# Second feed-forward product made transposed, its residual added by VectorE on the way out of PSUM

## The reference

```python
for l in range(3):
    scores = leaky_relu(si[:, :, None] + sj[:, None, :] + attn_b[l])   # si, sj: x times a vector
    attn = softmax(where(mask, scores, -inf))
    h  = layernorm(x + attn @ x, g1[l], beta1[l])
    ff = gelu(h @ W1[l] + b1[l]) @ W2[l] + b2[l]                       # 256 -> 1024 -> 256
    x  = layernorm(h + ff, g2[l], beta2[l])
```

## Time and profile before

| | us |
|---|---|
| median of 3 runs (lowest, highest) | 2346.72 (2340.11, 2352.82) |
| the profiled execution, own time | 2341.39 |
| its span, first to last instruction | 2339.6 |
| PE busy, share | 2266.7, 97% |
| PE weight loads (PEld) busy, share | 2100.0, 90% |
| DVE busy, share | 2081.9, 89% |
| ACT busy, share | 1678.3, 72% |
| POOL busy, share | 1101.6, 47% |
| granted TensorE clock, mean | 0.993 |

### The profile page before, as it was taken

How to read it: one execution, slowest core, us unless ns; L and a number is a source line. 1 busy time by engine, 2 the same in 40 slices (tenths; PEclk the granted TensorE clock), 3 DMA queues, 4 the chain that set the end, 5 groups by cost and what they waited for, 6 DMA issues and landing times.

```text
span 2339.6 us, 44738 instructions
## 1 busy us (share of the span) xinstructions
PE 2266.7 (97%) x15900; PEld 2100.0 (90%) x15900; DVE 2081.9 (89%) x4844; ACT 1678.3 (72%) x2682; POOL 1101.6 (47%) x1319
## 2 busy tenths in 40 slices
PE   8999999997899999999999999999999999999997
PEld 7988888896899999899999999999998999999996
DVE  5998999999798989989999999999898999999875
ACT  3444444334788888788888888988888878788784
POOL 3556666565253443443434345344344564653521
PEclk9999999999999999999999999999999999999998
DMA  5665555466979777787575665765666657566431
GB/s 164 183 197 168 154 158 169 134 185 204 235 204 233 213 208 195 216 221 207 172 248 158 186 205 172 205 184 171 183 194 217 176 159 216 163 190 179 122 106 46
DMA packets 282815, 427.00 MB, mean 183 GB/s; under 512 B 89376, under 2 KB 183264, under 8 KB 282592
## 3 DMA queue, kind: packets, MB, share of 16 engines
q1 hardware_dynamic: 254944, 323.47, 44.5%
q0 software_dynamic: 27648, 100.68, 18.7%
HBM read 226.65 MB, written 79.99 MB: 131 GB/s over the span
## 4 chain that ended last, share of the span: by engine, by line
PE 57%; DVE 17%; ACT 9%; POOL 6%; DMA 5%; issue 4%; SPq 1%; DVEq 0%; ACTq 0%; POOLq 0%
PE A L1928 6%; PE A L1929 5%; PE A L1930 5%; PE PT L1959 4%; PE PT L1955 4%; PE PT L1956 4%; DVE t L1600 4%; PE Y L1969 3%; PE Y L1970 3%; PE Y L1971 3%; DVE g_lo L1689 2%; PE A L45 2%; PE A L46 2%; PE A L47 2%; ACT t L1461 2%
## 5 line engine op out<-in xcount | busy, mean ns | idle before, releaser
L1928 PE MATMUL A<-x_hi,pT_hi 128*128 128x258 f32 x1536 | 439.8, 286 | 7.5 <-DVE u L1619 4.3
L1969 PE MATMUL Y<-w,g_hi 128*128 128x256 f32 x1536 | 438.0, 285 | 6.6 <-DVE g_lo L1689 5.5
L1929 PE MATMUL A<-x_hi,pT_lo 128*128 128x258 f32 x1536 | 434.1, 283 | 0.0
L1930 PE MATMUL A<-x_lo,pT_hi 128*128 128x256 f32 x1536 | 431.9, 281 | 0.0
L1970 PE MATMUL Y<-w,g_hi 128*128 128x256 f32 x1536 | 430.6, 280 | 0.0
L1971 PE MATMUL Y<-w,g_lo 128*128 128x256 f32 x1536 | 430.1, 280 | 0.0
L1507 ACT ACTIVATE g<-PT,b 128x512 f32<-128x512 f32 x384 | 263.8, 687 | 219.6 <-PE PT L1959 215.8
L1363 POOL DMA_DIRECT2D t<-maskT x192 | 173.4, 946 | 399.4 <-DVE t L1600 392.6
L1607 DVE TENSOR_TENSOR pT_lo<-t,pT_hi 128x512 fp32r<-128x512 f32 x384 | 256.8, 684 | 80.5 <-ACT t L1461 80.0
L1689 DVE TENSOR_TENSOR g_lo<-g,g_hi 128x512 fp32r<-128x512 f32 x384 | 262.9, 685 | 66.3 <-ACT g_hi L1510 66.1
L1969 PEld LDWEIGHTS Y<-w,g_hi 128*128 128x128 f32 x1536 | 289.3, 188 | 28.3 <-DVE g_lo L1689 11.9
(11 more groups left out here) (196 smaller groups left out, 5791.9 us busy)
## 6 DMA issues: line engine op xcount, KB each, us to landing
t<-maskT POOLq DMA_DIRECT2D x192, 512.0 KB, 4.6
mask<-mask SPq DMA_DIRECT2D x192, 256.0 KB, 4.4
a_adj_t<-in_adj SPq DMA_DIRECT2D x64, 512.0 KB, 4.4
maskT<-turned SPq DMA_DIRECT2D x64, 512.0 KB, 5.0
rrow<-rline SPq DMA_DIRECT2D x96, 256.0 KB, 4.9
x_rows<-rows SPq DMA_DIRECT2D x24, 1024.0 KB, 7.7
mask<-a_mask SPq DMA_DIRECT2D x64, 256.0 KB, 4.6
turned<-maskT SPq DMA_DIRECT2D x32, 512.0 KB, 6.9
```

What stands on the lines that cost most here:

```text
L1928: pe.matmul(L.A[:, t, 0:DE], hi, L.x_hi[par][:, j, :], start=(j == 0), stop=False)
L1929: pe.matmul(L.A[:, t, 0:DE], lo, L.x_hi[par][:, j, :], start=False, stop=False)
L1930: mm = pe.matmul(L.A[:, t, 0:D], hi, L.x_lo[par][:, j, :], start=False, stop=(j == NT - 1))
L1969: pe.matmul(L.Y[:, t, :], hi, w2_part(0, f), start=False, stop=False)
```

## The change

`down` is turned: W2's 128x128 pieces are the stationary operand and the gelu's output, 512 columns, is the moving one. Two banks of `Y`, now called `YT[0]` and `YT[1]`, hold the product transposed (features on partitions, 512 rows in the free dimension). `down` has 6 matmuls of 512 columns in place of 12 of 256, its first four wait for the gelu alone and its last two for `g_lo`. `residual` is gone. A new VectorE step `sum_z` reads both banks, adds `h` and writes `zT`, which lies in the buffer `xo` that `n2` fills later. A new PE step `transpose_z` turns `zT` back into rows in `Y` with 8 transposes, inside `aggregate` of the chunk two further on, before its step j = 2. `stats2`, and `end` for the last chunk, wait for these. Waits for the earlier store of `xo` move from `n2` to `sum_z`; `h` waits for `sum_z` of the chunk before.

```diff
@@ scalar
             if m >= 1:
                 act.wait_ge(L.s_ffn1, KF * m)
+                act.wait_ge(L.s_zT, KD * m)
...
             act.wait_ge(L.s_rs2, 4 * (m + 1))
-            if m >= 2:
-                act.wait_ge(L.s_xst, 16 * (m - 1))
@@ vector
+        def sum_z(m):
+            dve.wait_ge(L.s_ffn2, KF * (m + 1))
+            if m >= 2:
+                dve.wait_ge(L.s_xst, 16 * (m - 1))
+                if layer_of(m - 2) < LAYERS - 1:
+                    dve.wait_ge(L.s_uv, 2 * TC * (m - 1))
+            for i in range(KD):
+                dve.tensor_tensor(L.zT[m % 2][:, i, :], L.YT[i][:, :], L.h[:, i, :], ALU.add).then_inc(L.s_zT, 1)
+
         def stats2(m):
-                if t == 0:
-                    dve.wait_ge(L.s_ffn2, KF * (m + 1))
+                if t % 2 == 0:
+                    dve.wait_ge(L.s_zT_turned, 2 * m + t // 2 + 1)
...
+                if old:
+                    sum_z(k - 2)
                 if agg:
-                    for j in range(LEAD, LEAD + 2):
+                    for j in range(LEAD, LEAD + 3):
                         p_lo(k, j)
                 if old:
                     stats2(k - 2)
...
+            sum_z(K - 1)
             for pair in range(2):
                 end(pair)
@@ tensor, aggregate
             for j in range(NT):
+                if k >= 2 and j == 2:
+                    transpose_z(k - 2)
...
-        def residual(m):
...
+        def transpose_z(m):
+            pe.wait_ge(L.s_zT, KD * (m + 1))
             for t in range(TC):
                 for i in range(KD):
-                    pe.matmul(L.Y[:, t, i * P:(i + 1) * P], L.h[:, i, t * P:(t + 1) * P], L.ident[:, :],
-                              start=(t % 2 == 0 and i == 0), stop=False, is_transpose=True)
+                    mm = pe.transpose(L.Y[:, t, i * P:(i + 1) * P], L.zT[m % 2][:, i, t * P:(t + 1) * P], L.ident[:, :])
+                if t % 2 == 1:
+                    mm.then_inc(L.s_zT_turned, 1)
@@ tensor, down
+            pe.wait_ge(L.s_gelu, 2 * (n + 1))
+            for i in range(KD):
+                ds = slice(i * P, (i + 1) * P)
+                pe.matmul(L.YT[i][:, :], w2_part(0, f)[:, ds], hi, start=(f == 0), stop=False)
+                pe.matmul(L.YT[i][:, :], w2_part(1, f)[:, ds], hi, start=False, stop=False)
             pe.wait_ge(L.s_g_lo, n + 1)
-            for t in range(TC):
...
-                pe.matmul(L.Y[:, t, :], hi, w2_part(0, f), start=False, stop=False)
-                pe.matmul(L.Y[:, t, :], hi, w2_part(1, f), start=False, stop=False)
-                mm = pe.matmul(L.Y[:, t, :], lo, w2_part(0, f), start=False, stop=last and t % 2 == 1)
...
+            for i in range(KD):
+                ds = slice(i * P, (i + 1) * P)
+                mm = pe.matmul(L.YT[i][:, :], w2_part(0, f)[:, ds], lo, start=False, stop=(f == KF - 1))
+            mm.then_inc(L.s_ffn2, 1)
...
                 up(k - 1, 0)
                 up(k - 1, 1)
-                residual(k - 1)
...
+            transpose_z(K - 1)
```

More of the change, by code:

```diff
@@ L798, in layer_buffers @@
     L.A, L.G, L.Y, L.lines = mem.A, mem.G, mem.Y, mem.PT
+    L.YT = [mem.Y[:, 2 * i:2 * i + 2, :].rearrange("p a d -> p (a d)") for i in range(2)]
     L.half = sb("half", [P, TC])
@@ L859, in layer_buffers @@
     L.xo = [sb("xo0", [P, TC, D], F32, "probabilities"), sb("xo1", [P, TC, D], F32, "odd keys")]
+    L.zT = [xo[:, :, :].rearrange("p (i a) d -> p i (a d)", i=KD) for xo in L.xo]
     L.prod = sb("prod", [P, 2, D], F32, "probabilities")
@@ L918, in layer_buffers @@
     L.s_out = sem("out")
-    L.s_last_bank = sem("last_bank")
+    L.s_zT = sem("zT")
+    L.s_zT_turned = sem("zT_turned")
     L.s_end = sem("end_step")
@@ L1726, in end @@
             done = 1 + 12 * pair
-            dve.wait_ge(L.s_last_bank, pair + 1)
+            dve.wait_ge(L.s_zT_turned, 2 * K)
             for t in tiles:
@@ L1734, in end @@
             for t in tiles:
-                if t == 0:
-                    dve.wait_ge(L.s_xst, 16 * (K - 2))
                 dve.scalar_tensor_tensor(xo[:, t, :], L.Y[:, t, :], L.mv2[:, t, 0:1], L.g2[:, :], ALU.subtract,
@@ L1820, in rest @@
                 if agg:
-                    for j in range(LEAD + 2, NT - 1):
+                    for j in range(LEAD + 3, NT - 1):
                         p_lo(k, j)
@@ L1963, in down @@
             n = KF * m + f
-            pe.wait_ge(L.s_g_lo, n + 1)
-            last = f == KF - 1
-            for t in range(TC):
-                ts = slice(t * P, (t + 1) * P)
-                hi, lo = L.g_hi[:, n % G_RING, ts], L.g_lo[:, n % G_RING, ts]
-                pe.matmul(L.Y[:, t, :], hi, w2_part(0, f), start=False, stop=False)
-                pe.matmul(L.Y[:, t, :], hi, w2_part(1, f), start=False, stop=False)
-                mm = pe.matmul(L.Y[:, t, :], lo, w2_part(0, f), start=False, stop=last and t % 2 == 1)
[L1972 to L1975, removed]
+            if f == 0:
+                if m == 0:
+                    pe.wait_ge(stage.s_z, SLOTS)
+                else:
+                    pe.wait_ge(L.s_n2, TC * m)
+            hi, lo = L.g_hi[:, n % G_RING, :], L.g_lo[:, n % G_RING, :]
+            pe.wait_ge(L.s_gelu, 2 * (n + 1))
[3 more added lines that the diff above has]
+                pe.matmul(L.YT[i][:, :], w2_part(1, f)[:, ds], hi, start=False, stop=False)
+            pe.wait_ge(L.s_g_lo, n + 1)
+            for i in range(KD):
+                ds = slice(i * P, (i + 1) * P)
+                mm = pe.matmul(L.YT[i][:, :], w2_part(0, f)[:, ds], lo, start=False, stop=(f == KF - 1))
+            mm.then_inc(L.s_ffn2, 1)
         def beside(slot):
@@ L1992, in rest @@
                     aggregate(k)
+                if k == K:
+                    transpose_z(K - 2)
                 up(k - 1, 0)
                 up(k - 1, 1)
-                residual(k - 1)
                 for f in range(KF):
```

## The result

The changed kernel takes 2393.88 us (median of 4 runs, 2389.59 to 2402.25) against 2343.91 us of the kernel before (4 runs, 2340.11 to 2352.82): ratio 1.0217, 95% interval 1.0189 to 1.0245, so 2.2% slower. The forecast was 2407, the range 2374 to 2440. The profiled execution takes 2393.82 us, its span is 2392.0 against 2339.6.

The account below looks back on a forecast made before the run. The prediction took PE as the bound, with a chain through ACT and DVE within 0.2 us of its pace. Terms 29 + 23.5 + 4 + 9 = 65.5 us on 2341.4 gave 2407 us, range 2374 to 2440.

Parts of the forecast that it names:

- The chain of the first two layers: Low part, additions, transposes, then j = 2: +1.15 us in 29 of 33 iterations, 36.7 us against 35.57; sum +29.
- The four long ones: Four iterations of the first two layers, long because of transfers that the new wait partly hides: −1 us each.
- The additions: sum_z on DVE, two additions out of PSUM a chunk: 2 × 0.67 = 1.34 us, ends 1.2 and 1.5.
- `down` and the weight loads: down on PE: 1.38 us in both forms, half as many weight loads buy nothing; 0.1 us gained an iteration.
- The rival on weight loads: Weight loads set PE's pace, so sum_z hides: 2333 us, not slower; chance 0.11 with its weaker form.
- The last layer: 13 iterations, gelu held by POOL's late nmr: nine times 2.1 us and four times 1.15, +23.5.
- the two terms: Last layer where nmr is late: additions 1.34 us plus transposes 0.79 us, the whole 2.1 us stays.
- The clock: Last layer: PE's wait of about 2.7 us lowers the clock in half of 13 iterations, 1.5 us each, +9.
- the signs of being right: PE waits once an iteration before transpose_z, 1.3 to 1.5 us, last layer 2 to 3; iterations 36.7 and 38 us.
- The prediction's rival for the first two layers: Clock falls there too, half of 33 iterations losing 1.5 us: +25, so 2432 us; chance 0.21.
- a microsecond there is hidden: Delay of n2 behind stats2 costs nothing, as down(0) needs n2 only some 4 us after up(0) begins.
- The end: Last two chunks have no aggregate beside them; sum_z and transposes stand bare, 2.1 us twice: +4.

Follow-up runs that it names:

- Run 4: Kernel before plus the two additions (result unused) behind the third low part, PE waiting for them before j = 2; down and transposes as before; 2382.41 us.
- run 1: Changed kernel with the eight transposes of zT before step j = 3 of aggregate in place of j = 2; 2373.56 us.
- run 10: run 6 with row_top moved behind the last low part on DVE; 2355.0 us.
- run 9: Changed kernel with its two additions made twice; 2484.51 us.
- run 5: Changed kernel with its two additions made three times; 2599.76 us.
- run 2: Changed kernel with the additions in row_top's place on DVE and row_top behind the third low part; 2378.3 us.
- run 6: run 2 with the statistics of the second norm one low part earlier on DVE; 2367.48 us.

## Why the prediction was right, and where it failed

*The chain of the first two layers: right to 0.14 us at each point.* From the first of the three `down` (1220.72), with the forecast in brackets: low part ends at 7.82 (7.82), additions at 9.02 (9.16), j = 2 begins at 9.92 (9.95), `up(0)` at 18.54 (18.50), and the iteration is 1257.49 − 1220.72 = 36.77 (36.7). That the end fits better than the parts is luck: the additions came 0.14 early, and from their end to j = 2 it took 0.90 in place of 0.79. PE's wait itself was forecast too long: "about 1.4 us" is the whole of the additions, while the prediction's own points give 9.16 − 8.01 = 1.15, and 0.98 was measured. In 33 iterations +27.6 (29). The four long ones became 5.6 us shorter together (38.26, 39.48, 37.71 and 38.82 became 37.36, 37.74, 36.77 and 36.79; forecast 4): the new wait did hide part of the transfers. Runs 4 and 1 show the cause: the additions with PE's wait, without the rest of the change, make most of the loss, and moving only the place where PE waits takes 20 us back.

*The additions: 0.68 each, 1.28 for the pair* (forecast 1.34), since the second starts before the first has ended.

*`down` and the weight loads.* 1220.72 to 1222.10 is 1.38 us, as forecast. PEld fell from 33.42 us in an iteration to 31.13 in run 10, and the iteration stayed at 35.6, so the loads did not set the pace. The rival on weight loads is out. The Trainium skill ("Perfetto Trace Analysis", section "Identifying the Most-Contended Engine") takes the busy share of the weight loads, beside the share of peak arithmetic, as the measure of TensorE's headroom. From the kernel before to run 10 that share fell from 94% to 87% of the iteration and gave no time; the matmuls' own 1.38 us told it.

*The last layer: +21.4 against 23.5, by the mechanism named.* Timeline of POOL in one of its iterations; then of PE, from that iteration's `up(0)` on, with its first matmul after each wait (the last row opens the next iteration); then the window on the iteration, and ACT's wait for `nmr` in the whole layer:

```profile
1958.35 2.92 POOL L1330 TENSOR_TENSOR nmr<-nm,rstd 128x4 f32<-128x4 f32 x1
```

```profile
1945.08 0.40 PE L1966 MATMUL PT<-h_hi,w 128*128 128x512 f32 x1
...
1969.20 0.36 PE L1942 MATMUL A<-x_hi,pT_hi 128*128 128x258 f32 x1 [0.48 <-DVE pT_lo L1609]
...
1973.96 1.09 PE L1951 MATMUL Y<-ident,xo 128*128 128x128 f32 x8 [1.25 <-DVE xo L1642]
...
1986.76 0.50 PE L1966 MATMUL PT<-h_hi,w 128*128 128x512 f32 x1 [0.42 <-ACT g_hi L1512]
```

```profile
1945.08:1983.42 38.34, 36.45 (x212) 31.08 (x210) 34.69 (x74) 29.02 (x47) 21.00 (x19) 1.00 0.59 177
```

```profile
ACT u L1484 <- POOL nmr L1330: 18.3, 9, 2.0
```

`nmr` took 2.92 us in nine iterations, as before, and ended 16.2 us after `up(0)` (1945.08 to 1961.27), as before: POOL's chain did not come forward. ACT waited 18.3 us for it in the layer, 12.5 before. Eight of the nine came to 38.3 to 38.8 us, 2.0 to 2.5 over 36.34; the ninth and the four with `nmr` early to 36.2 to 37.5. Run 4, in which the transposes stay behind `up(1)`, parts the two terms: against the changed kernel it is 0.1 us shorter in the first two layers (36.72), where moving the transposes was forecast to cost nothing, and 0.8 shorter in the last (37.53), where their 0.79 was forecast to stay.

*The clock: the term that failed, +9 forecast, 0 measured.* The step is "In the last layer PE's wait grows to about 2.7 us". I had put all of the lost time (38.4 less 35.6) into one wait. The iteration did reach 38.3, but PE was off work for only 38.34 − 36.45 = 1.9 us of it, and that is spread: 0.48 before j = 0, 1.25 before the transposes, the rest in gaps under 0.15; its busy time was 36.45 and not 35.6. The longest wait for the additions in the layers is 1.3 us there (2 to 3 stood among the signs of being right), 1.6 in the whole run, and PEclk stays at 1.00. The price and the kind were right: run 9 makes waits of nearly that size (2.6 us) in ten iterations of the last layer and loses the clock in all ten, and a fall costs 39.7 − 38.1 = 1.6 us, near the 1.5 taken. The Trainium skill ("TensorE: Matmul & The Clock Gate", section "HAM oscillation — how this bites in real kernels") tells of a loop with a wait of some 3 to 5 us in each round, which brings the clock down in every round. The runs agree at that size and go below it: a fall in every iteration of the first two layers at 3.5 to 3.6 us (run 5), in 11 of 30 at 2.1 to 2.3 (the first iteration left out) and in all ten at 2.6 (run 9), and in none at up to 1.3 (the changed kernel). The prediction's rival for the first two layers leaned on this loop with waits of 1.4 us, less than half of the loop's; that section of the Trainium skill does not say that such waits bring the clock down, and here they did not.

*The second norm: "a microsecond there is hidden" held only just.* The prediction looked for the next user of `n2` at `down(0)`, 4 us after `up(0)` begins. But gelu 0 stands behind `n2` on ACT, and `up(2)`, which begins 2.9 us after `up(0)`, waits for it. Timeline of ACT of the kernel before, in the iteration of the earlier trace rows: second norm, table load, gelu 0, without a pause.

```profile
1226.55 1.92 ACT L1489 ACTIVATE xo<-Y,nmr,rstd 128x256 f32<-128x256 f32 x4
1228.49 1.28 ACT L1507 ACT_TABLE_LOAD   x1
1229.78 0.69 ACT L1507 ACTIVATE g<-PT,b 128x512 f32<-128x512 f32 x1
```

ACT's wait grew from 3.4 to 58.1 us, and it was hidden because the first chain was longer still. Runs 1 and 2 took that away and stood at 36.27, where run 10 shows that PE alone needs 35.63. In eight iterations of the changed kernel POOL's `ve` took 1.62 us, and `up(2)` came 0.4 to 0.6 us late: 3.6 us in all that the forecast did not have.

*The end: +4.9 against 4.* Before the layers the changed kernel was 1.5 us ahead, for which I have no cause.

The sum: 27.6 + 21.4 + 4.9 − 1.5 = 52.4 against 65.5. Of the 13.1 too many, 9 are the clock. Without that term the forecast would have been 2398 us, against 2394 measured.

## What to carry to other kernels

Work that is equal in columns on the bounding engine is not equal in place: the eight transposes were moved from a stretch where they covered a gelu to a place behind two new additions, in a chain with 0.2 us to spare. Of the additions' 1.28 us 1.0 to 1.2 showed in each iteration, and in the last layer the transposes' 0.8 with it. Before taking a chain apart, ask which chain lies just below it; here two experiments that freed the first both stopped at the second, 0.6 us short of PE's own pace. And split a lost time by the waits it will fall into before pricing the clock: one wait of 2.7 us and several that add to 2 cost differently.

## What the runs showed of the hardware that was not expected

POOL's tiny operations have a few fixed durations, not a spread. Min, median and max in ns of `ve` (47 times) in the changed kernel, in run 6 and in run 10:

```profile
L1336 POOL TENSOR_TENSOR ve<-mv,eps x47: 476/483/1619, 641.4 to 2348.8; 128x4 f32<-128x4 f32 x47
```

```profile
L1336 POOL TENSOR_TENSOR ve<-mv,eps x47: 474/484/2223, 639.1 to 2324.6; 128x4 f32<-128x4 f32 x47
```

```profile
L1336 POOL TENSOR_TENSOR ve<-mv,eps x47: 475/485/2830, 648.7 to 2314.3; 128x4 f32<-128x4 f32 x47
```

It takes 0.48 us if it gets through while DVE changes from one low part to the next, and else, but for one of 1.08, 1.62 (changed kernel, 8 times), 2.22 (run 6, 15 times) or 2.83 (run 10, 4 times); these 27 all end some 0.05 us after `row_top` has ended on DVE; yet, short or long, it starts 0.22 to 0.25 us into a low part. `nmr` has 0.52, 1.52 and 2.92 for the most part, and also ends some 0.05 us after an instruction of DVE. The Trainium skill ("SBUF — State Buffer", section "Who interferes with whom") says that a VectorE instruction with two inputs in SBUF contends with a GpSimd instruction that reads SBUF, since its second input comes through a read interface that the two share, and that the shared ports are an exclusive lock. The low parts and `row_top` are of that kind, and the trace agrees: the long operations take 1.14 to 2.35 us more than the short ones and end with DVE's instructions. Not each change of instruction on DVE lets POOL through: in run 6 the one to `row_top` did not. What decides it stays open. So an edit of DVE's order changed how often and for how long POOL was held, and with it when ACT loads its table and PE goes on.
